# Sorting 200,000 edges by window: one scattered record per edge, against blocks of 2,000 edges placed by a product and added to rows of 16

## The reference

```
edge_weight [200000], x [12500, 256]
feats  = relu(x @ w1 + b1) @ w2 + b2                          # per head, 64 wide
hid    = relu([feats[src], feats[dst], weight] @ a1 + ab1)    # 129 wide
e      = leaky_relu(hid @ a2 + ab2, 0.2);  w = exp(e - max(e))
pooled = segment_sum(w * feats[dst], src);  row_sum = segment_sum(w, src) + 1e-10
out    = layernorm(x + concat over heads(pooled / row_sum))
```

## Time and profile before

| | us |
|---|---|
| median of 3 runs | 6067.9 (6063.4 to 6071.91) |
| the profiled execution | 6098.69 |
| its span | 6096.9 |
| PE busy | 4346.8 (71%) |
| DVE busy | 4243.0 (70%) |
| POOL busy | 3789.0 (62%) |
| ACT busy | 3138.2 (51%) |

### The profile page before, as it was taken

The page is one execution under the profiler, slowest core; times in us unless marked ns, Lnnn a source line. Parts: engine busy times, 40 slices in busy tenths (PEclk is TensorE's granted clock), DMA queues, the critical chain, the costliest instruction groups (busy, mean ns, idle before and its releaser), DMA issues.

```text
span 6096.9 us, 127641 instructions
## 1 busy us (share of the span) xinstructions
PE 4346.8 (71%) x24741; PEld 3053.9 (50%) x24742; DVE 4243.0 (70%) x23832; ACT 3138.2 (51%) x10707; POOL 3789.0 (62%) x3738
## 2 busy tenths in 40 slices
PE   3645555454555546189999999999999999999940
PEld 1423333332333323066667766676676766666630
DVE  7644444444444444378888888888888888888863
ACT  0211111111111111078888888888888888888842
POOL 6878777778777877745555555555555555555532
PEclk9867777776777777599999999999999999999975
...
DMA packets 298498, 833.67 MB, mean 137 GB/s; under 512 B 113010, under 2 KB 152050, under 8 KB 298342
## 3 DMA queue, kind: packets, MB, share of 16 engines
...
## 4 chain that ended last, share of the span: by engine, by line
PE 36%; POOL 31%; issue 16%; ACT 6%; DMA 4%; DVE 4%; DVEq 0%; another core or an unknown queue 0%; SPq 0%; POOLq 0%; ACTq 0%
POOL records L556 31%; PE psum L753 15%; PE psum L740 9%; PE psum L757 9%; ACT z L850 4%; DMA out_dram<-z 3%; PE psum L766 2%; DVE z L1179 2%; DMA p_win<-p_table 1%; PE psum L777 1%; ACT onehot L879 1%; DVE acc L976 1%; ACT onehot_t L868 1%; DVE z L1169 1%; DVE acc L1228 1%
## 5 line engine op out<-in xcount | busy, mean ns | idle before, releaser
L587 POOL DMA_INDIRECT z<-qf_table,rec x1664 | 1598.1, 960 | 1565.9 <-PE psum L740 926.7
L556 POOL DMA_INDIRECT records<-z x1600 | 1942.5, 1214 | 503.5 <-issue 503.5
L850 ACT ACTIVATE z<-z 128x64 f32<-128x64 f32 x6656 | 1651.2, 335 | 56.7 <-ACT z L857 28.8
L753 PE MATMUL psum<-p_win,onehot_t 128*128 x9984 | 1438.0, 277 | 235.8 <-issue 128.0
L753 PEld LDWEIGHTS psum<-p_win,onehot_t 128*128 128x128 bf16 x9984 | 965.9, 97 | 805.3 <-issue 488.5
L740 PE MATMUL psum<-z,onehot 128*128 128x260 f32 x3328 | 1027.2, 391 | 2.6 <-DVE acc L1228 1.6
L757 PE MATMUL psum<-z,ident 128*128 128x258 f32 x3328 | 1006.6, 384 | 0.0
L1179 DVE SCALAR_TENSOR_TENSOR z<-z,a_b 128x129 f32<-128x129 f32 x3328 | 888.9, 290 | 0.0
L1179 DVE SCALAR_TENSOR_TENSOR z<-psum,a_b 128x129 f32<-128x129 f32 x3328 | 820.8, 282 | 3.3 <-issue 3.3
L651 PE MATMUL psum<-z,ones_b 125*128 125x400 bf16 (+1 forms) x1600 | 344.3, 310 | 656.2 <-DVE z L968 656.1
L1169 DVE TENSOR_TENSOR z<-z,psum 128x258 f32<-128x258 f32 x1664 | 690.3, 415 | 117.3 <-PE psum L757 87.0
...
## 6 DMA issues: line engine op xcount, KB each, us to landing
qf_table<-acc SPq DMA_DIRECT2D x100, 378.9 KB
p_table<-acc SPq DMA_DIRECT2D x100, 377.9 KB
p_win<-p_table SPq DMA_DIRECT2D x100, 377.9 KB
z<-qf_table,rec POOLq DMA_INDIRECT x1664
records<-z POOLq DMA_INDIRECT x1600
...
```

What stands on the lines that cost most here:

```text
L556: pool.indirect_dma_start(out=records, out_offset=bass.IndirectOffsetOnAxis(ap=pos_at[0:EP, s, c:c + 1], axis=0), in_=rec_out[0:EP, s, 4 * ...
L587: pool.indirect_dma_start(out=z_t[:, o + j, :], out_offset=None, in_=qf_table, in_offset=bass.IndirectOffsetOnAxis(ap=rec[:, o + j, 3:4].b ...
L753: mm = pe.matmul(to, onehot_t[:, j, :], p_flat[:, bass.ds((w % 2) * (3 * ZW) + (part * ZW + o), n)], start=(part == 0), stop=(part == 2 an ...
L850: op = act.activation(z_t[:, slot, o:o + DO], z_t[:, slot, o:o + DO], ACT.Copy, scale=z_t[:, slot, o + DO:o + HF])
```

## The change

The records are no longer scattered one edge at a time. A block is now 16 columns (2,000 edges), and there are 100 blocks. The array is cut into chunks of 16 places (`S`); a row of the new array `sorted_rows` is one chunk: 16 places by 6 numbers (`NF`: row in the window, the destination node in two digits, the weight in three bfloat16 parts). For each block:

- ACT makes the one-hot rows over the windows, one block ahead (`windows`: 16 activations of 100 columns and 4 of 400).
- PE puts the block's own base (a count made beforehand, in two bfloat16 parts) and the in-column count into PSUM by three products of 400 columns per 4 columns of edges (`prefix`).
- DVE picks the places of four columns by one product and one sum over it (`pick`), splits them into chunk and slot (`split`), makes `placed`, the fields laid at their slot (`slots`, a 256-wide and a 1,536-wide product), and 16 one-hot rows over the 320 chunks that a block can touch (`chunks`).
- PE multiplies the two, 16 products that sum in one PSUM bank to 96 by 320 (`place`). ACT copies it out (`take_sum`), PE turns it (`turn_rows`), DVE copies it out and works out the row number of each of the 320 chunks (`row_ids`).
- POOL issues 3 indirect transfers (128, 128 and 64 rows of 384 bytes) that add to `sorted_rows`, which SP has filled with zeros at the start. It issues them after all transfers of the block before have landed, since a chunk can be touched by two blocks.

The base of each block needs the window counts of every column, so `hist_take` now reads out the counts of each half group on DVE, where before they summed in PSUM; after them come 16 transposes, 15 running additions and some 30 small instructions. At the end a new loop of 13 rounds (`BULK`) reads `sorted_rows` (SP, 128 by 768 numbers a round), turns it by 6 products on PE, writes the four words of each record (DVE, ACT), and stores `records` (SP). The array of window starts that the table needs (`win_iota`) is made by POOL behind its last scatter. In the node work, the transposes of the features ride in the `qf` product (386 columns where 258 were), and ACT takes over a copy of 256 columns that DVE did. The loops over groups become `sort_loop`, with one more group of 4 blocks at the end for what is still in the pipe. The second stage is untouched.

```diff
-    CPI = EC // GROUPS
-    SUBS = 4
-    LOT = CPI // SUBS
+    CB = 16
+    BLOCKS = EC // CB
     CH = 4
-    CHUNKS = LOT // CH
-    assert N == WN * W and E == EP * EC and CPI * GROUPS == EC and CHUNKS * CH * SUBS == CPI
+    PER = BLOCKS // GROUPS
+    S = 16
+    NF = 6
+    SF = S * NF
+    KC_MAX = 320
+    KB = [128, 128, 64]
...
+    sorted_rows = nc.dram_tensor("sorted_rows", (CHUNKS + 3 * P, SF), F32, kind="Internal").ap()
...
+            rows_g = sorted_rows[0:CHUNKS, :].rearrange("(g t c) n -> g t (c n)", t=P, c=P // S)
+            def load_stage(g):
+                since(sp, s_field_mm, g - 1)
+                sp.dma_start(stage[:, g % 2, :], rows_g[g, :, :]).then_inc(s_stage[g % 2], 16)
+            load_stage(0)
+            for g in range(BULK):
+                if g + 1 < BULK:
+                    load_stage(g + 1)
+                sp.wait_ge(s_field_a, g + 1)
+                sp.wait_ge(s_field_b, g + 1)
+                sp.dma_start(rec_d[:, g * P * 4:(g + 1) * P * 4], rec_all[:, g * P:(g + 1) * P, :].rearrange("p t n -> p (t n)")).then_inc(s_rec_st, 16)
+            sp.wait_ge(s_rec_st, 16 * BULK)
...
-                for s in range(SUBS):
-                    pool.wait_ge(s_at, g * 2 * SUBS + 2 * s + 2)
-                    pool.sem_inc(s_passed, 1)
-                    for c in range(LOT):
-                        pool.indirect_dma_start(
-                            out=records, out_offset=bass.IndirectOffsetOnAxis(ap=pos_at[0:EP, s, c:c + 1], axis=0),
-                            in_=rec_out[0:EP, s, 4 * c:4 * c + 4], in_offset=None, compute_op=ALU.bypass).then_inc(s_scat[s], 16)
-            loop(pool, GROUPS, scatter)
+                for b in range(PER):
+                    if live_b(g, b, -3):
+                        h = g * PER + (b - 3)
+                        pool.wait_ge(s_row_i, h + 1)
+                        since(pool, s_scat, h * 48)
+                        pool.sem_inc(s_passed, 1)
+                        for k in range(3):
+                            pool.indirect_dma_start(
+                                out=sorted_rows, out_offset=bass.IndirectOffsetOnAxis(ap=row_i[0:KB[k], (b - 3) % 2, k:k + 1], axis=0),
+                                in_=rows_out[0:KB[k], (b - 3) % 2, 2 * (W + 1) + k * SF:2 * (W + 1) + (k + 1) * SF], in_offset=None, compute_op=ALU.add).then_inc(s_scat, 16)
+            sort_loop(pool, scatter)
+            pool.wait_ge(s_sum, 4 * BLOCKS)
+            pool.iota(win_iota, [[P, NT]], base=0, channel_multiplier=0, allow_small_or_imprecise_dtypes=True).then_inc(s_win_iota, 1)
...
             def prefix(g, q):
-                n = g * (CPI // CH) + q
+                n = g * (PER * 4) + q
                 pe.wait_ge(s_oh, n + 1)
-                since(pe, s_carry, n)
-                o = psum[:, q % 2, :]
-                for c in range(CH):
-                    oh = win_oh[0:EP, q % 2, c, :]
-                    pe.matmul(o[:, (c + 1) * W:(CH + 1) * W].rearrange("p (c w) -> p c w", w=W), ones_b[0:EP, :],
-                              oh.unsqueeze(1).to_broadcast([EP, CH - c, W]), start=(c == 0), stop=False, skip_group_check=True)
-                    mm = pe.matmul(o[:, c * W:(c + 1) * W], before[0:EP, :], oh, start=False, stop=(c == CH - 1),
-                                   skip_group_check=True)
-                mm.then_inc(s_count, 1)
+                since(pe, s_pos, n - 1)
+                o = psum[:, q % 2, 0:CH * W]
+                own = ident_b[0:BLOCKS, bass.ds(g * PER + q // 4, 1)].to_broadcast([BLOCKS, P])
+                at = slice(q % 4 * CH * W, (q % 4 + 1) * CH * W)
+                pe.matmul(o, own, base_hi[0:BLOCKS, at], start=True, stop=False)
+                pe.matmul(o, own, base_lo[0:BLOCKS, at], start=False, stop=False)
+                pe.matmul(o, before[0:EP, :], win_oh[0:EP, q // 4 % 2, q % 4 * CH:(q % 4 + 1) * CH, :].rearrange("p c w -> p (c w)"),
+                          start=False, stop=True).then_inc(s_count, 1)
+            def place(g, b, j):
+                n = (g * PER + (b - 2)) * 4 + j
+                pe.wait_ge(s_chunks, n + 1)
+                if j == 0:
+                    pe.wait_ge(s_placed, g * PER + (b - 1))
+                    since(pe, s_sum_ev, g * PER + (b - 2))
+                for c in range(j * CH, (j + 1) * CH):
+                    mm = pe.matmul(psum[0:SF, 7, 0:KC_MAX], placed[0:EP, b % 2, c, :], chunk_oh[0:EP, b % 2, c, :],
+                                   start=(c == 0), stop=(c == CB - 1))
+                mm.then_inc(s_sum, 1)
+            def turn_rows(g, b):
+                h = g * PER + (b - 3)
+                pe.wait_ge(s_sum_ev, h + 1)
+                since(pe, s_row_f, h)
+                since(pe, s_f_ev, min(g * 2 + b // 2 * 2, GROUPS * 2) if isinstance(g, int) else g * 2 + b // 2 * 2)
+                for k in range(3):
+                    pe.matmul(psum[0:KB[k], 4, 2 * (W + 1) + k * SF:2 * (W + 1) + (k + 1) * SF], chunk_t[0:SF, k * P:k * P + KB[k]], ident_b[0:SF, 0:SF], start=True, stop=True)
+                own = ident_b[0:BLOCKS, bass.ds(h, 1)].to_broadcast([BLOCKS, P])
+                for u in range(3):
+                    mm = pe.matmul(psum[:, 4, 0:2 * (W + 1)], own, step_p[0:BLOCKS, u, :], start=(u == 0), stop=(u == 2))
+                mm.then_inc(s_turned, 1)
...
+            def windows(g, b, j):
+                n = (g * PER + b) * 4 + j
+                since(act, s_pos, n - 7)
+                for c in range(j * CH, (j + 1) * CH):
+                    op = act.activation(win_oh[0:EP, b % 2, c, :], iota_win[0:EP, 0, :], ACT.Abs, scale=-1.0,
+                                        bias=edge_win[0:EP, bass.ds((g * PER + b) * CB + c, 1)])
+                op.then_inc(s_win_dist, 1)
+                act.wait_ge(s_win_dist, n + 1)
+                own = win_oh[0:EP, b % 2, j * CH:(j + 1) * CH, :].rearrange("p c w -> p (c w)")
+                act.activation(own, own, ACT.Relu, scale=-1.0, bias=ones_f[0:EP, 0:1]).then_inc(s_oh, 1)
+            def take_sum(g, b):
+                h = g * PER + (b - 3)
+                act.wait_ge(s_sum, h * 4 + 4)
+                since(act, s_turned, h)
+                act.activation(chunk_t[0:SF, :], psum[0:SF, 7, 0:KC_MAX], ACT.Copy).then_inc(s_sum_ev, 1)
...
+            def pick(g, b, j):
+                n = (g * PER + b) * 4 + j
+                dve.wait_ge(s_count, n + 1)
+                since(dve, s_pos, n)
+                dve.tensor_tensor(picked[0:EP, :, :], psum[0:EP, j % 2, 0:CH * W].rearrange("p (c w) -> p c w", c=CH),
+                                  win_oh[0:EP, b % 2, j * CH:(j + 1) * CH, :], ALU.mult).then_inc(s_picked, 1)
+                dve.wait_ge(s_picked, n + 1)
+                dve.tensor_reduce(place_f[0:EP, b % 2, j * CH:(j + 1) * CH], picked[0:EP, :, :], AX_X, ALU.add).then_inc(s_pos, 1)
+            def split(g, b):
+                h, r = g * PER + (b - 1), (b - 1) % 2
+                dve.wait_ge(s_pos, h * 4 + 4)
+                dve.tensor_copy(place_i[0:EP, :], place_f[0:EP, r, :]).then_inc(s_split, 1)
+                dve.wait_ge(s_split, h * 4 + 1)
+                dve.tensor_scalar(chunk_i[0:EP, :], place_i[0:EP, :], S.bit_length() - 1, None, ALU.logical_shift_right).then_inc(s_split, 1)
+                dve.tensor_scalar(slot_i[0:EP, :], place_i[0:EP, :], S - 1, None, ALU.bitwise_and).then_inc(s_split, 1)
+                dve.wait_ge(s_split, h * 4 + 3)
+                dve.tensor_scalar(chunk_f[0:EP, :], chunk_i[0:EP, :], float(-(KC_MAX // 2)), None, ALU.add)
+                dve.tensor_copy(slot_b[0:EP, :], slot_i[0:EP, :]).then_inc(s_split, 1)
+            def slots(g, b):
+                h, r = g * PER + (b - 1), (b - 1) % 2
+                dve.wait_ge(s_split, h * 4 + 4)
+                dve.tensor_tensor(slot_oh[0:EP, :, :], slot_b[0:EP, :].unsqueeze(2).to_broadcast([EP, CB, S]),
+                                  iota_s[0:EP, :].unsqueeze(1).to_broadcast([EP, CB, S]), ALU.is_equal).then_inc(s_slots, 1)
+                dve.wait_ge(s_slots, h + 1)
+                since(dve, s_sum, h * 4 - 4)
+                dve.tensor_tensor(placed[0:EP, r, :, :].rearrange("p c (s f) -> p c s f", f=NF),
+                                  slot_oh[0:EP, :, :].unsqueeze(3).to_broadcast([EP, CB, S, NF]),
+                                  fields[0:EP, bass.ds(h * CB, CB), :].unsqueeze(2).to_broadcast([EP, CB, S, NF]), ALU.mult).then_inc(s_placed, 1)
+            def chunks(g, b, j):
+                h, r = g * PER + (b - 1), (b - 1) % 2
+                dve.wait_ge(s_split, h * 4 + 4)
+                since(dve, s_sum, h * 4 + (j - 7))
+                for c in range(j * CH, (j + 1) * CH):
+                    op = dve.tensor_scalar(chunk_oh[0:EP, r, c, :], iota_k[0:EP, :], chunk_f[0:EP, c:c + 1], None, ALU.is_equal)
+                op.then_inc(s_chunks, 1)
+            def row_ids(g, b):
+                h, r = g * PER + (b - 3), (b - 3) % 2
+                dve.wait_ge(s_turned, h + 1)
```

(22 more changed lines are left out.)

648 lines of the change are left out of this document (403 added, 245 removed).

## The result

The changed kernel takes 5837.5 us (median of 4 runs, 5820.7 to 5843.8) beside 6067.8 for the kernel before on the same chip: ratio 0.9616, 95% interval 0.9595 to 0.9638. It is faster by 3.8%. The forecast was 5,343 us with a range of 5,180 to 5,640, so the sign was right and the size was missed by 494 us, beyond the range. The span of the profiled execution is 5838.7 us. Chips differ a little: the kernel before takes 6067.8 us on this chip, 6091.7 on that of e1 to e4, 6095.5 on that of e5 to e8 and 6114.4 on that of e9 and e11.

The account below looks back on a forecast made before the run. POOL's scatter issue bounds the sort; afterwards DVE should. Loop start 184, 100 blocks of 15.5 us (1,550), 112 to stage two and 3,522 carried over give 5,368 us span, 5,343 after 0.5% off; range 5,180 to 5,640.

Parts of the forecast that it names:

- What bound before: Sort of the kernel before: POOL's 1,600 scatters, one every 1.52 us, set the pace, with node work hidden beside them.
- A block on each engine: Block loop, work per block: DVE 14.8 us, PE 12.4 at clock 1.00, ACT 10.7, POOL 7.6 with its landing; DVE longest.
- the first rival: DVE's comparisons run at four columns a cycle, 0.16 us each: 14.4 us a block, 5,235 us; chance 0.27.
- Waits of the engines for each other: Block loop: DVE waits for PE 2.8 us a group, 0.7 a block, making a block 15.5 us.
- its own signs: Block loop: forecast fails if a block takes under 14 or over 17 us; DVE should be over 85% busy.
- `window` waits for `p_sum`: Second part of a group: the next `prefix` stands behind `window` on PE, costing DVE some 0.7 us in three places.
- The second, longer waits: Block loop: longer waits, an in-between clock or one-column comparisons give 17 to 19 us a block, 5,490 to 5,690; chance 0.18.
- The third, PE at its lower level: Block loop: PE granted 1.2 GHz throughout, 24.8 us a block, 6,268 us, slower by 3%; chance 0.03.
- The fourth: Block loop: adding scatters land so late that POOL's chain bounds, felt beyond 11 us of landing; chance 0.04.
- The start: Before the block loop: -7 edge arithmetic, +40 reading out counts, +22 behind the histogram; loop starts at 184 us, not 128.4.
- The end: Last block to stage two: 7 + 6 us drain, 49 newly on the path, 45 for 13 rounds of 3.5, 5 more.
- Stage two: From the end of the sort to the kernel's end: unchanged, carried over as 3,522 us.

Follow-up runs that it names:

- e1: Changed kernel with SP issuing the qf_table store of a window before its p_table store: 5563.6 us, ratio 0.9132.
- e4: Changed kernel with each of the 16 comparisons of a block done twice, once into a spare buffer: 6062.4 us, ratio 0.9954.
- e5: The changed kernel as it is, timed again on another chip: 5868.1 us, ratio 0.9629.
- e8: The edits of e6 and e7 together, on top of e1: 5407.3 us, ratio 0.8874.
- e9: e8 with POOL's five long instructions on the weights moved beside the histogram: 5407.4 us, ratio 0.8836.
- e11: e8 with every comparison done twice, in all blocks but the last: 5653.0 us, ratio 0.9248.
- e2: Changed kernel with ACT issuing the qf_table store itself, right behind its copy: 5562.7 us, ratio 0.9129.
- e6: e1 with DVE adding the bias to the p product ahead of its step's pick, into one of two buffers: 5479.0 us, ratio 0.8992.
- e3: Changed kernel with the transfers to sorted_rows writing where they added: 5889.3 us, ratio 0.9668.
- e7: e1 with small transfers and win_iota before the loop, clearing of acc halved with POOL, sorted_rows read through four buffers: 5508.2 us, ratio 0.9038.

## Why the prediction was wrong

The prediction's sum was 5,368 us of span; 5,838.7 were measured, 471 more. That is +10 at the start, +461 in the loop, +34 at the end and -35 in stage two, when the loop is counted from ACT's first one-hot rows (193.3) to 2205. The forecast then took 0.5% off, 27 us, because the profiled execution of the kernel before was that much longer than its median; after the change the two agree (5840.5 and 5837.5). These 27 us and the -35 of stage two seem to be one thing, a slower chip under the first profile, so they nearly cancel in the 494.

**What bound before.** Right. POOL's 1,600 scatters are gone, and the start of stage two moved from 2575.0 to 2351 us.

**A block on each engine: right.** DVE 14.0 us (forecast 14.8), ACT 1087.00 over the stretch or 10.9 (10.7). PE's busy time is 14.4 at a mean granted clock of 0.86; forecast were 12.4 at 1.00, and 12.4 / 0.86 is 14.4. (In e1 it is 13.6 at 0.95, where the same division gives 13.1, so the exact match is in part luck.) The comparison, which had no row, was put at 0.24 from start to start:

```profile
829.21 0.93 DVE L1320 TENSOR_SCALAR acc<-z 125x320 bf16<-125x320 bf16 x4
```

One lasts 0.30, so three distances are 0.93 - 0.30 = 0.63, and a distance is 0.21. That lies about midway between the 0.25 by the cast in the earlier trace rows, two columns a cycle, and the 0.16 by which the first rival went. The Trainium skill (VectorE: DVE Perf Modes, the perf-mode tier table) gives four columns a cycle, for 2,048 columns; this trace does not show that for 320 columns with the scalar read from SBUF. The comparisons cost 3.4 us a block where 3.9 were forecast and the first rival had 2.6. DVE's work came out between the two (14.0; forecast 14.8, rival 13.5), and the time went by neither.

**Waits of the engines for each other, "0.7 us a block": this step failed.** It measured 6.1, and by its own signs the forecast fails with it: a block of over 17 us (20.1), and DVE busy less than 85% of the loop (70%). The forecast matched the engines' work step by step, PE against DVE, and found little to wait for. It left out that the node work is coupled to the sort by buffers and by SP's in-order program. Of the 5.4 us missed, 3.1 are the store (e1, and e2 by another way), 0.9 the late sum in front of PE's next window (e6). The forecast named this second one, with "`window` waits for `p_sum`", but priced it in three places a group at 0.7, as if DVE met it alone; PE's wait for it alone is 305.9 us in the loop, 4.1 each time. 1.4 more remain in e8, of which the experiments don't tell the parts. With both removed a block is 16.1 to 16.2, inside the 14.9 to 16.5 that the forecast gave its likeliest case.

The trace of the kernel before had the sign. In the earlier trace rows its L1064, the DVE copy that the change moves to ACT, shows no wait; but the same line, summed over us 400 to 2400 of that trace, waited for the `qf_table` store:

```profile
L1064 DVE COPY acc<-psum 125x256 f32<-125x256 f32 x83 | 34.7, 418 | 52.8 <-DMA qf_table<-acc 52.8
```

ACT's own copy of the tile (L829) waited another 38.4 us for the same store. 52.8 us in 2,000 were harmless there: a group took 97 us, and DVE waited 697.4 us in the same stretch for old scatters to land. The hand-written order gives the rest: SP issues the `qf` store behind the `p` part of step 12, and step 13 of the same group wants the buffer back. In between lies one step, 3.9 us by the forecast, and the store needs 10.8. A change that makes the steps shorter makes such a distance short.

**Rivals.** The second, longer waits, was the right kind at too small a size: 17 to 19 us a block against 20.1. The third, PE at its lower level through the loop, fell: the mean granted clock of the loop was 0.86, nearer to the level of 2.4 GHz than to that of 1.2, and 0.95 in e1, where the waits for the store are gone. The fourth fell with e3, although its sign was there: the forecast said that it fails if POOL still waits for landings when its row numbers are ready, and POOL did so 24 times, 211.6 us. It cost the loop nothing. Its landing was well sized: 3.3 us in the median against the 3 taken. The issue was not: 1.56 + 0.3 us for each scatter, where 1.52 had been carried over from the earlier trace rows; that cost nothing in the loop.

**The start: +10 us.** Larger errors nearly cancelled here, which is luck. The histogram went without POOL beside it, since POOL waits for the 17th edge step, and lost none of the 28 us kept for it. But a half group took 2.05 us, 1.12 more than the 0.93 of before, where 0.81 were allowed for reading out its counts: +15. So the histogram took 102 us (40.9 to 143.0) where the terms give 115. Behind it the running additions, put at 4.5, took 22.7 beside POOL, +18; the copies of 1,600 and 512 columns took 3 more than their 8.3, and the rest about 2. By e9 the contention costs 18 to 20 us in either place, so the 28 us stood at a wrong place and were 8 to 10 too many.

**The end: +34 us.** The drain was put at 7 + 6 us. The chain from the last pick to the tile numbers took 44.6:

```profile
2233.54 0.57 DVE L1329 COPY z<-psum 128x394 f32<-128x394 f32 x1 [8.48 <-DMA sorted_rows<-z]
...
2248.30 1.09 DVE L1389 TENSOR_SCALAR acc<-acc,z 100x1664 bf16<-100x1664 f32 x1 [12.90 <-POOL acc L658]
...
2271.82 21.73 DVE L1440 MEMSET acc<- 128x26000 f32 x1 [11.66 <-issue]
...
2293.60 0.38 DVE L1447 COPY z<-psum 128x128 f32<-128x128 f32 x1
```

With nothing left to lie beside them, three blocks leave the pipe one after another, DVE waits 8.48 us for a landing, and then 12.90 us for POOL, whose `iota` stands behind six scatters. Counted from 2205 this is 43.3 us for 13, or +30. Some 7 of it is the `qf` store again: ACT's last copy waits for it until 2214.8, and in e1 the same chain takes 37.4 us (1898.7 to 1936.1). From 2248.3 to the end of the clearing at 2293.6 are 45.3 us; the 49 carried from the earlier trace rows were about right, and the claim that this cost moves onto the path was the best of the prediction. The 13 rounds took 52 us, 4.1 each, not 3.5. That sum was mis-sized in its parts too: the products of a round take 2.7 us in e7 and not 1.3, and one of its two terms of 2 us has no row. e7 takes 55 us of this stretch away again (141 in e1, 86 in e7).

**Stage two** was carried over as 3,522 and showed 3,487; e5, e1 and e3 put its gathers at 3,261 to 3,266 us, the kernel before at 3,263.7. So the term was right.
